# A local attention mask moved from matmuls on TensorE to an add on VectorE

## The reference

```python
x = L0_attn_x
xn = _layernorm(x)
x = x + local(xn) + routed(xn)

# local: 16 query heads, 4 key heads, head size 32, rmsnorm and rope on q and k
scores = einsum('bhqd,bhkd->bhqk', q, k) * scale
mask = (key > query) | (abs(query - key) > 64)
attn = softmax(where(mask, -10000.0, scores))
local = (attn @ v) @ Wo.T + bo

# routed: each token picks one of 16 key/value heads; causal softmax over all 1024 keys
```

## Time and profile before

| | |
|---|---|
| median of 3 runs | 668.64 us (667.66 to 670.04) |
| the profiled execution | 671.4 us, of which its span (first to last instruction) is 669.5 us |
| TensorE clock granted, mean of the span | 0.993 |
| PE busy | 637.4 us, 95% of the span |
| DVE busy | 455.8 us, 68% |
| ACT busy | 361.7 us, 54% |
| POOL busy | 442.4 us, 66% |

### The profile page before, as it was taken

How to read it: one execution, slowest core, us unless ns; L and a number is a source line. 1 busy time by engine, 2 the same in 40 slices (tenths; PEclk the granted TensorE clock), 3 DMA queues, 4 the chain that set the end, 5 groups by cost and what they waited for, 6 DMA issues and landing times.

```text
span 669.5 us, 19210 instructions
## 1 busy us (share of the span) xinstructions
PE 637.4 (95%) x7432; PEld 509.8 (76%) x7432; DVE 455.8 (68%) x1184; ACT 361.7 (54%) x906; POOL 442.4 (66%) x384
## 2 busy tenths in 40 slices
PE   4699999999999999999999899999999999999997
PEld 3587788887888888888778677777777777777675
DVE  3966457657665675656664388887878787878454
ACT  5357355625544445535257455656565565656684
POOL 3876856368654749382895467776878687868730
PEclk9999999999999999999999899999999999999999
DMA  9524222241223133212216631503214131302011
GB/s 315 197 60 112 60 77 79 76 122 41 78 70 91 50 94 104 78 39 75 64 33 166 163 96 58 137 26 93 71 51 113 51 111 36 104 29 89 4 34 33
DMA packets 64939, 56.59 MB, mean 85 GB/s; under 512 B 6480, under 2 KB 48848, under 8 KB 64848
## 3 DMA queue, kind: packets, MB, share of 16 engines
q1 hardware_dynamic: 62704, 54.45, 27.9%
q10 hardware_dynamic: 2144, 0.93, 0.5%
HBM read 37.20 MB, written 17.89 MB: 82 GB/s over the span
## 4 chain that ended last, share of the span: by engine, by line
PE 88%; DVE 5%; ACT 2%; DMA 2%; issue 2%; SPq 0%; ACTq 0%; DVEq 0%
PE gemm L946 20%; PE s_ps L1055 12%; PE od_ps L1104 11%; PE st_ps L1088 10%; PE gemm L1032 7%; PE gemm L942 6%; PE od_ps L1118 5%; PE win L1006 4%; PE win L991 3%; PE s_ps L1127 2%; PE av L1018 2%; DMA raw<-w_tok 2%; PE av L1045 1%; PE tp L957 1%; PE tp L913 1%
## 5 line engine op out<-in xcount | busy, mean ns | idle before, releaser
L946 PE MATMUL gemm<-w_tok,xt 128*128 128x512 f32 (+1 forms) x768 | 184.0, 380 | 5.4 <-DVE g_exp L1188 2.2
L946 PEld LDWEIGHTS gemm<-w_tok,xt 128*128 128x128 f32 x768 | 129.6, 191 | 28.5 <-DVE g_exp L1188 2.7
L1055 PE MATMUL s_ps<-k_stack,w_tok 96*128 96x512 f32 (+2 forms) x336 | 100.0, 381 | 0.3 <-DVE x_res L1286 0.3
L1088 PE MATMUL st_ps<-w_tok,k_stack 98*128 98x512 f32 x288 | 98.9, 413 | 0.2 <-ACT p_loc L1545 0.2
L1545 ACT ACTIVATE p_loc<-st_ps 128x512 f32<-128x512 f32 x144 | 77.6, 599 | 35.9 <-PE st_ps L1088 34.7
L1321 DVE TENSOR_REDUCE picked_fk<-s_ps 128x1 f32<-128x512 f32 x112 | 72.3, 684 | 9.0 <-PE s_ps L1055 8.9
L1497 ACT ACTIVATE p_loc<-win,l_max 128x96 f32<-128x96 f32 x256 | 60.9, 390 | 31.1 <-DVE l_max L1260 31.1
L1055 PEld LDWEIGHTS s_ps<-k_stack,w_tok 96*128 96x128 f32 x336 | 54.9, 188 | 24.6 <-issue 8.8
L1642 POOL TENSOR_TENSOR rope_b<-qkv,sin_t 128x128 f32<-128x128 f32 (+1 forms) x32 | 27.5, 880 | 65.5 <-DVE qkv L1238 65.5
L1666 POOL TENSOR_TENSOR p_loc<-p_loc,l_rec 128x1536 f32<-128x1536 f32 x16 | 44.1, 2758 | 36.4 <-DVE l_rec L1272 36.4
L1324 DVE CUSTOM_DVE_ANT_0 s_ps<-s_ps,x_ln,picked_fk 128x128 f32<-128x128 f32 (+3 forms) x112 | 56.8, 555 | 9.7 <-PE s_ps L1055 9.7
(11 more groups left out here) (172 smaller groups left out, 1295.4 us busy)
## 6 DMA issues: line engine op xcount, KB each, us to landing
w_tok<-q_parts SPq DMA_DIRECT2D x72, 128.0 KB, 2.6
q_parts<-qt SPq DMA_DIRECT2D x120, 64.0 KB
x_ln<-x SPq DMA_DIRECT2D x8, 512.0 KB, 4.6
x_res<-x SPq DMA_DIRECT2D x16, 256.0 KB, 2.8
partial<-x_res SPq DMA_DIRECT2D x16, 256.0 KB, 2.3
w_tok<-partial SPq DMA_DIRECT2D x8, 512.0 KB, 5.2
raw<-w_tok SPq DMA_DIRECT2D x3, 1024.0 KB, 12.5
v_win<-v_rows SPq DMA_DIRECT2D x64, 48.0 KB, 2.2
```

Of the source, the lines that this page charges most:

```text
L946: i = e.matmul(g[:, 0:cols], xs[l][:, k, a * P:(a + 1) * P], w_tok_p[r][:, k, c0:c0 + cols], start=first, stop=last)
L1055: e.matmul(s_ps[bank][:, 0:cols], q_op[b][0:HALVES, i, h, :], k_stack[0:HALVES, b * S + c0:b * S + c0 + cols], start=True, stop=True).then ...
L1088: e.matmul(st_ps[k % ST_BANKS][:, :, :], k_stack[0:HALVES + 2, b * S + j * P:b * S + (j + 1) * P], q_op[b][0:HALVES + 2, i, :, :], start=T ...
```

## The change

The mask matmuls go, and with them `l_rows`, its source `rows`, its DMA and its conversion. A step `masked` is put between `scores` and `maxima`: one DVE instruction reads all four banks of `win` (128x1536), adds `l_mask` (broadcast over the four key heads, now plain fp32) and writes `p_loc`. The maxima are taken from `p_loc`, and the exponentials read and write `p_loc` in place. `win` is released by `masked` instead of by the exponentials; the wait for the transposes that last read `p_loc` goes from ACT (`weights`) to DVE (`masked`), and the wait for the mask from PE to DVE. The planner has new costs for the three steps, so the whole list of the first stage, and what follows from its times in the second, is made anew.

```diff
         for g in range(HKV):
-            p.take(("win", g), ("scores", m, a, g), ("p_exp", (m, a, g)))
+            p.take(("win", g), ("scores", m, a, g), ("masked_s", (m, a)))
             win_free[g] = None
         do("scores", m, a)
-        yield 1.6, []
+        yield 1.0, []
+        do("masked", m, a)
+
+        def masked_end(end):
+            win_free[:] = [end + HOP] * HKV
+        yield 0, [("V", 1.65)], masked_end
         do("maxima", m, a)
         yield 0, [("V", 1.75)]
         do("weights", m, a)
-        def exps_end(end):
-            win_free[:] = [end - 1.1 * (HKV - 1 - g) + HOP for g in range(HKV)]
-        yield 0, [("A", 4.4)], exps_end
+        yield 0, [("A", 4.0)]
...
-    l_mask = sb(one, "l_mask", [P, 2, QUADS * KEYS], F32R)
-    l_rows = sb(one, "l_rows", [P, REP, QW], F32R)
+    l_mask = sb(one, "l_mask", [P, 2, QUADS * KEYS])
...
                 if i == 0:
                     lane.wait_ge(*M["filled"].of("all"))
-                    lane.wait_ge(*M["masks"].of("all"))
...
                         mm = e.matmul(win[:, g, quad * KEYS:(quad + 1) * KEYS],
                                       q_t[d, a, quad, :, :].rearrange("p h q -> p (h q)"), k_t[d, k0:k0 + KEYS],
-                                      start=True, stop=False)
-                    for g in range(HKV):
-                        d, keys = slice(g * DK, (g + 1) * DK), slice(quad * KEYS, (quad + 1) * KEYS)
-                        mm = e.matmul(win[:, g, keys], l_rows[d, :, :].rearrange("p h q -> p (h q)"),
-                                      l_mask[d, int(i > 0), keys], start=False, stop=True)
+                                      start=True, stop=True)
...
+            elif step == "masked":
+                m, a = key
+                lane.wait_ge(*M["s_mm"].of((m, a)))
+                lane.wait_ge(*M["masks"].of("all"))
+                if m:
+                    lane.wait_ge(*M["pt_mm"].of((m - 1, a, QUADS - 1)))
+                seen = l_mask[:, int((2 * m + a) % IT > 0), :].unsqueeze(1).to_broadcast([P, HKV, QUADS * KEYS])
+                e.tensor_tensor(p_loc[a][:, :, :, :].rearrange("p g s k -> p g (s k)"), win[:, :, 0:QUADS * KEYS], seen,
+                                ALU.add).then_inc(*M["masked_s"].did((m, a)))
...
             elif step == "maxima":
                 m, a = key
-                lane.wait_ge(*M["s_mm"].of((m, a)))
+                lane.wait_ge(*M["masked_s"].of((m, a)))
...
-                e.tensor_reduce(l_max[:, a, :].rearrange("p (g s) -> p g s", g=HKV),
-                                win[:, :, 0:QUADS * KEYS].rearrange("p g (s k) -> p g s k", s=QUADS), AX.X, ALU.max,
+                e.tensor_reduce(l_max[:, a, :], p_loc[a][:, :, :, :].rearrange("p g s k -> p (g s) k"), AX.X, ALU.max,
...
             elif step == "masks":
                 lane.wait_ge(*M["mask_in"].of("all"))
-                e.activation(l_mask[:, :, :], mask_t[:, :, :], ACT.Copy).then_inc(*M["masks"].did())
-                e.activation(l_rows[:, :, :], rows_t[:, :, :], ACT.Copy).then_inc(*M["masks"].did("all"))
+                e.activation(l_mask[:, :, :], mask_t[:, :, :], ACT.Copy).then_inc(*M["masks"].did("all"))
...
             elif step == "weights":
                 m, a = key
                 lane.wait_ge(*M["s_max"].of((m, a)))
-                if m:
-                    lane.wait_ge(*M["pt_mm"].of((m - 1, a, QUADS - 1)))
...
-                        i = e.activation(p_loc[a][:, g, quad, :], win[:, g, quad * KEYS:(quad + 1) * KEYS], ACT.Exp,
+                        i = e.activation(p_loc[a][:, g, quad, :], p_loc[a][:, g, quad, :], ACT.Exp,
                                          bias=l_max[:, a, n:n + 1])
...
             elif step == "late_constants":
-                e.dma_start(mask_t[:, :, :], mask).then_inc(*M["mask_in"].did(inc=16))
-                e.dma_start(rows_t[:, :, :].rearrange("p h q -> p (h q)"), rows).then_inc(
-                    *M["mask_in"].did("all", inc=16))
+                e.dma_start(mask_t[:, :, :], mask).then_inc(*M["mask_in"].did("all", inc=16))
```

More of the change, by code:

```diff
@@ L704 @@
     "g_sum_r g_top_r picked_fk picked_fv fk_hi fk_lo fk_dup fv_out qt_hi q_stored0 q_stored1 q_last0 q_last1 fk_mm fk_out "
-    "v_pad v_out0 v_out1 v_in0 v_in1 q_t_mm q_t_r k_t_mm k_t_r s_mm s_max p_exp masks l_sum l_rec p_r pt_mm "
+    "v_pad v_out0 v_out1 v_in0 v_in1 q_t_mm q_t_r k_t_mm k_t_r s_mm masked_s s_max p_exp masks l_sum l_rec p_r pt_mm "
     "p_t_r pv_mm at_hi at_lo wo_mm res_bias res_r res_in0 res_in1 res_stored0 res_stored1 "
@@ L710, with mixed_attention_kernel @@
 ).split()
-def mixed_attention_kernel(nc, counts, x, w_tok, w_qt, w_o, b_qkv, b_o, w_norm, scale, rope, ident, mask, rows, rank,
+def mixed_attention_kernel(nc, counts, x, w_tok, w_qt, w_o, b_qkv, b_o, w_norm, scale, rope, ident, mask, rank,
                            out):
@@ L787, in mixed_attention_kernel @@
     mask_t = sb(over, "mask_t", [P, 2, QUADS * KEYS])
-    rows_t = sb(over, "rows_t", [P, REP, QW])
     over.close()
@@ L1910 @@
         "mask": local_mask(),
-        "rows": np.tile(np.eye(QW, dtype=np.float32), (HKV, REP)),
         "rank": (H - np.arange(H, dtype=np.float32))[None, :],
```

## The result

The changed kernel takes 690.83 us (median of 4 runs, 690.25 to 696.27), the kernel before 669.34 on the same chip: a ratio of 1.034, 95% interval 1.0309 to 1.0371. It is 21.5 us slower, where 664.1 was predicted, and lies outside the range. The profiled execution is one of 690.25 us with a span of 689.0. One execution of a later run (e4) took 1028 us at a granted clock of 0.56 and counts in no ratio.

The account below looks back on a forecast made before the run. PE was taken to bound the first stage, busy 322.0 of 330.0 us. Masks off PE, -8.0, and waits for busier DVE, +3.5, sum to -4.5 us: median 668.64 to 664.1, range 658.5 to 670.6.

Parts of the forecast that it names:

- What the busier DVE costs PE: First stage: PE's added waits for DVE, which has 28.3 us more work; 3.5 us taken, between 2.5 and 5.0.
- The chain of a tile: Local attention: a tile's weights come 1.6 us later, covered by slack even at the last tile; counted as nothing.
- The earlier release: `win` freed after the add, some 5.5 us earlier, can only make scores and transposes start earlier; counted as nothing.
- The list made anew: First stage's new step order: no term, only in a rival where all gain is kept, 660.6 to 658.5 us, chance 0.16.
- The masks off PE: Scores blocks on PE: removing 256 mask matmuls gives back 0.5 us a tile, 8.0 us, bounds 7.0 and 10.2.
- The add: New DVE step before the maxima: 1.77 us a tile, 28.3 us more on DVE in all.
- The maxima: DVE maxima reading SBUF instead of PSUM: 1743 ns instead of 1753, counted as nothing.
- The exponentials: On ACT, from SBUF instead of PSUM: 0.3 us a tile more, bounds 0.27 and 3.4; hidden.
- The second stage: The routed stage, 282.5 us long: the change adds and removes nothing; as long as before within 1.5 us.
- The slower one: Rival: add and maxima block a `gemm` bank, PE waits 1.4 us a tile; 10 to 12 tiles give 675 to 677; chance 0.14.

Follow-up runs that it names:

- e4: The kernel before, no instruction changed, its list planned anew with measured costs for scores and exponentials: 687.3 us, ratio 1.028.
- e5: The kernel before, masks kept on PE, with only the add put in ahead of the maxima, its result overwritten: 688.2 us, ratio 1.029.
- e1: The changed kernel's instructions in the list of the kernel before, add and maxima together where the maxima stood: 682.8 us, ratio 1.020.
- e6: The kernel before in its own list, without the mask matmuls and nothing in their place: 661.8 us, ratio 0.989.
- e13: e6 plus an idle 1536-element reduce on DVE behind each tile's maxima, its result read by nobody: 676.1 us, ratio 1.009.
- e7: e1 with the exponentials reading `win` in PSUM again and releasing it: 681.7 us, ratio 1.019.
- e2: The changed kernel, its list planned with measured costs for scores, add and exponentials: 679.2 us, ratio 1.016.
- e12: The kernel before, no instruction changed, planner's scores cost 1.55 instead of 1.6 us, so two steps change places: 668.5 us, ratio 0.999.
- e8: The changed kernel with the exponentials of the last two tiles moved behind copies that PE had waited for: 688.3 us, ratio 1.031.
- e17: e13 with the idle reduce over 768 elements instead of 1536: 665.9 us, ratio 0.996.
- e16: The kernel before in its own list, masks on PE as 4 matmuls of 384 columns a tile instead of 16 of 96: 666.0 us, ratio 0.995.
- e9: e1 with the sums taken by ACT as accumulated outputs of the exponentials instead of by DVE reduces: 697.8 us, ratio 1.041.

## Why the prediction was wrong

**The step that failed is "What the busier DVE costs PE".** It put 3.5 us (2.5 to 5.0) on 28 us of new DVE time. In the unchanged list the add costs 18.9 to 19.8 (e5), and the whole change has a stage 18.7 us longer than the kernel without masks (e1 less e6). PE's idle time in the stage rose by 18.4 us, from 10.7 to 29.1, where some 3.5 were foretold; not all of it is behind DVE. Both readings behind it were of the wrong kind. That three of sixteen sums stood in the chain of before says how well the *old* list hides the steps that it was made for; a step that it doesn't know comes on top. And the growth of waits with load was applied to PE's 8 us of idle time, which were the remainder of a good order, not the waits of a random one. Of the cost, 10.6 us are the term as it was meant, DVE's time (e13 less e6); it was mis-sized threefold.

**"The chain of a tile" failed too: 1.6 us later, "still covered", counted at nothing.** The cover was read from PE's side alone: transposes that never waited. But ACT and DVE take their steps in order, and ACT stood 31.1 us at the exponentials already; that time was called ACT's own. With the add in the old list it is 50 us, and behind it stand copies that PE needs. Where `win` is released by the exponentials, the place costs 7.2 us (e7 less e13); in the change, place, longer exponentials and earlier release together cost 8.2 (e1 less e13). The earlier release, which "can only make scores and transposes start earlier", did take away the waits for `win` that e7 has, but with the longer exponentials the time stayed (e1 against e7). One reading was wrong besides: the 2.9 and 2.0 us of the earlier trace rows are idle time of the weight loads (PEld); before its matmuls on `win` PE itself never idled. No term hangs on that.

**The list made anew had no term.** It was mentioned only as what might make the gain larger. In place of the old list it cost 8.0 us more (690.8 less e1's 682.8; 11.0 by the stage), and e2 shows 3.6 us less for another one.

**What held.** The masks off PE: 0.42 us a tile and 6.6 us of time where 8.0 was said, just under its lower bound of 7.0; the stage shows 8.0 against the profile of before and 6.4 against e12's. 0.42 us for 16 matmuls are 26 ns each. By the floor of 25 ns that the Trainium skill gives (page "TensorE: Matmul & The Clock Gate", section "Wait — 56ns, not 53.3ns?") it was to be 6.4, so the page came nearer than the start-to-start reading of 30 ns. The add: 1752 ns, 1.77 us said. The maxima: 1743, as said. The exponentials: 0.53 us a tile more where 0.3 was taken, within the bounds; what they cost in time was not measured by itself. The second stage: unchanged.

**The rivals.** The slower one named the mechanism that e13 and e1 show, add and maxima in front of a bank's read, with 1.4 us where 1.82 and 1.94 are seen; but it asked for 10 to 12 blocked tiles, gave 675 to 677, and had 0.14. What it lacked is what the later chain costs, and the list.

What stays open is how the 8.2 us beyond DVE's time come about in the change: the steps that carry them differ from tile to tile, and no run takes them singly. Why the new list is worse than the old one is open too; its waits are known, but e8 shows that removing two of them moves them elsewhere.

## What to carry to other kernels

Where several engines run one fitted order, an engine's free time is no room: price a new step by inserting an idle one of its length in the same order (e13, e17), and once more in the place that it will have, since the place can cost nearly as much again (8.2 us with all that the change adds there, beside 10.6). Before the order is planned anew, try the change in the old one, and the old instructions in a new one: e4's 19 us are nearly as much as the whole loss of the change. If the cost on the bounding engine is one of instruction count, make the instructions wider there (e16) before moving the work to another engine.

## What the runs showed of the hardware

**A DVE instruction with two SBUF operands held up POOL.** It shows in the start-up and goes with the spread of the first `scores`. In e6:

```profile
34.42 1.27 POOL L1622 TENSOR_TENSOR qkv<-qkv,rms_y 128x640 f32<-128x640 f32 x1
...
37.14 2.29 DVE L1138 TENSOR_TENSOR w_o<-raw,w_o 128x2048 fp32r<-128x2048 f32 x1 [0.95 <-ACT w_o L1394]
```

And in e13:

```profile
34.40 2.29 DVE L1139 TENSOR_TENSOR w_o<-raw,w_o 128x2048 fp32r<-128x2048 f32 x1 [0.95 <-ACT w_o L1399]
34.77 3.04 POOL L1627 TENSOR_TENSOR qkv<-qkv,rms_y 128x640 f32<-128x640 f32 x1
...
37.87 0.66 PE L958 MATMUL tp<-idt,qkv 128*128 128x128 f32 x4 [3.98 <-POOL qkv L1627]
```

The same POOL instruction takes 3.04 us where DVE began first, and ends 1.1 us after DVE does (37.81 and 36.69); alone it takes 1.27. PE waits 3.98 us for it, and the first `scores` come at 44.74 instead of 41.37. All 19 profiles divide in this way: in the nine where DVE began first the POOL instruction took 3.0 to 3.1 us and the first `scores` came at 44.5 to 45.4; in the ten others it took 1.3 us, and they came at 41.3 to 42.9. This is as the Trainium skill has it (page "SBUF — State Buffer", section "SBUF: two separate sides"): for a VectorE instruction with two SBUF inputs and a GpSimd instruction that reads SBUF, the two share a pair of ports, and whichever begins first holds it for the whole instruction. A start that falls one way or the other moves the first `scores` by 1.6 to 4.1 us, more than the difference of e7 from e1 or of e12 from before.

**An accumulated output of an activation** cost 0.09 us for each exponential (0.36 instead of 0.27 us apart), with a read of the accumulator that is an instruction of 187 ns in the trace (e9).
